# One block of sixteen value products per key tile instead of two of eight, in a two-layer conditioned attention on one Trainium2 core

## What is computed

```python
xn = layer_norm(x, norm_w, norm_b)
q = (xn @ q_w + q_b).reshape(Bx, Tx, H, -1)
k = (xn @ k_w + k_b).reshape(Bx, Tx, H, -1)
att = jnp.einsum('bnhl,bmhl->bnmh', q, k)
att = att + (1.0 - mask) * -1000000.0
att = jax.nn.softmax(att, axis=2)
v = ((xn @ v_w + v_b) * src_mask[:, :, None]).reshape(Bx, Tx, H, -1)
y = jnp.einsum('bnmh,bmhl->bnhl', att, v).reshape(Bx, Tx, Dx)
```

## Time and profile before

| | us |
|---|---|
| median of 3 runs | 675.45 |
| lowest and highest | 674.78, 677.27 |
| span of the profiled execution, first to last instruction | 674.4 |
| PE busy | 589.8 (87%) |
| DVE busy | 470.1 (70%) |
| ACT busy | 347.5 (52%) |
| POOL busy | 53.5 (8%) |

### The profile page before, as it was taken

How to read it: one execution, slowest core, us unless ns; L and a number is a source line. 1 busy time by engine, 2 the same in 40 slices (tenths; PEclk the granted TensorE clock), 3 DMA queues, 4 the chain that set the end, 5 groups by cost and what they waited for, 6 DMA issues and landing times.

```text
span 674.4 us, 9341 instructions
## 1 busy us (share of the span) xinstructions
PE 589.8 (87%) x2922; PEld 241.6 (36%) x2922; DVE 470.1 (70%) x905; ACT 347.5 (52%) x409; POOL 53.5 (8%) x42
## 2 busy tenths in 40 slices
PE   1989888999999999999999999999889666999666
PEld 1464412222222222222222222222234553588655
DVE  4639996888788788788888788888020547585652
ACT  1565304564655656656656655656976421538021
POOL 7224600000000000000000000000000005000000
PEclk9999955999999999999999999999989896999969
DMA  8188801500600600600410330100000000000003
GB/s 228 51 142 205 338 21 31 65 0 4 96 1 3 95 0 3 93 2 3 70 25 3 52 43 3 57 7 3 2 1 1 0 0 1 0 1 1 0 1 124
DMA packets 20021, 29.95 MB, mean 44 GB/s; under 512 B 5202, under 2 KB 11556, under 8 KB 19844
## 3 DMA queue, kind: packets, MB, share of 16 engines
q1 hardware_dynamic: 19996, 29.62, 20.8%
HBM read 21.02 MB, written 8.60 MB: 44 GB/s over the span
## 4 chain that ended last, share of the span: by engine, by line
PE 62%; DVE 23%; ACT 9%; issue 4%; DMA 1%; SPq 0%; DVEq 0%; ACTq 0%
PE bank L539 18%; PE bank L519 15%; DVE halfmax L749 15%; PE bank L500 14%; PE bank L581 11%; ACT work L391 3%; DVE stats L708 2%; ACT work L425 2%; DVE y_all L788 1%; PE bank L552 1%; DVE work L722 1%; DVE parts L722 1%; PE bank L524 1%; ACT parts L408 1%; DMA vecs<-in_mask_BxS_ff 1%
## 5 line engine op out<-in xcount | busy, mean ns | idle before, releaser
L749 DVE TENSOR_REDUCE halfmax<-bank 128x1 f32<-128x512 f32 x512 | 325.7, 688 | 63.7 <-PE bank L519 63.5
L425 ACT ACTIVATE work<-bank 128x1024 f32<-128x1024 f32 x256 | 250.0, 1023 | 152.6 <-PE bank L581 152.3
L519 PE MATMUL bank<-ks,qs 99*128 (+1 forms) x512 | 202.9, 404 | 17.1 <-DVE halfmax L749 11.0
L581 PE MATMUL bank<-qs,ks 102*128 (+1 forms) x512 | 167.6, 386 | 7.9 <-ACT work L425 5.4
L539 PE MATMUL bank<-work,vs 128*32 128x512 f32 x1024 | 137.0, 608 | 0.4 <-ACT yT L433 0.4
L519 PEld LDWEIGHTS bank<-ks,qs 99*128 (+1 forms) x512 | 49.7, 97 | 228.4 <-DVE halfmax L749 125.3
L581 PEld LDWEIGHTS bank<-qs,ks 102*128 (+1 forms) x512 | 47.5, 100 | 61.2 <-ACT work L425 18.5
L500 PE MATMUL bank<-parts,work 128*128 128x256 f32 x192 | 44.6, 393 | 7.1 <-ACT work L391 7.1
L500 PEld LDWEIGHTS bank<-parts,work 128*128 128x128 f32 x192 | 37.7, 198 | 13.4 <-ACT work L391 7.6
L367 POOL COPY vs<-v_all 128x512 f32 (+1 forms) x8 | 4.9, 612 | 396.8 <-PE bank L539 396.8
L500 PE MATMUL bank<-work,y_all 128*128 128x512 f32 x64 | 30.9, 624 | 2.4 <-ACT work L391 2.4
(11 more groups left out here) (119 smaller groups left out, 406.1 us busy)
## 6 DMA issues: line engine op xcount, KB each, us to landing
part_rows<-parts SPq DMA_DIRECT2D x8, 768.0 KB, 5.0
qs<-part_rows SPq DMA_DIRECT2D x48, 128.0 KB
ks<-part_rows SPq DMA_DIRECT2D x48, 128.0 KB
xs<-in_x SPq DMA_DIRECT2D x2, 1024.0 KB, 6.1
out_x<-xs SPq DMA_DIRECT2D x4, 512.0 KB, 2.9
parts<-in_L_cond_emb_w SPq DMA_DIRECT2D x1, 1024.0 KB, 5.6
parts<-in_L_cond_W_emb SPq DMA_DIRECT2D x1, 1024.0 KB, 7.9
ks<-in_mask_BxSx_fk SPq DMA_DIRECT2D x1, 1024.0 KB, 4.8
```

The lines of the kernel that those rows point to most:

```text
L425: act.activation(prob[:, c % 2, j, :], sT[u % 2][:, :], ACT.Exp).then_inc(exp_done, 1)
L519: pe.matmul(o, qs[0:ROW_MAX, slot, j, qt * P:(qt + 1) * P], ks[0:ROW_MAX, slot, j, n * HALF:(n + 1) * HALF], start=True, stop=True).then_i ...
L581: last = pe.matmul(sT[u % 2][:, n * HALF:(n + 1) * HALF], ks[0:ROWS, slots[0], j, c * P:(c + 1) * P], qs[0:ROWS, slots[0], j, n * HALF:(n ...
L749: dve.tensor_reduce(halfmax[:, r, n:n + 1], src, axis=AX.X, op=ALU.max, negate=True).then_inc(sN_read, 1)
```

## The change

The value products of both query halves of a tile are now issued together, after head 1, as one block of eight source matmuls (sixteen MATMUL records). The turns that went with the two blocks go with the one: 4 before it, 4 after it. The number of instructions, their operands and the `pv_done` increment stay the same.

```diff
-                        if c > 0 and j % 2 == 1:
-                            turns(VALUES_TURNS // 2)
-                            values(g, c - 1, j // 2)
-                            turns(VALUES_TURNS // 2)
-                        if c == 0 and not first and 1 <= j <= NH:
-                            turns(VALUES_TURNS // 2)
-                            values(g - 1, NT - 1, j - 1)
-                            turns(VALUES_TURNS // 2)
+                        if j == 1 and (c > 0 or not first):
+                            turns(VALUES_TURNS // 2 * NH)
+                            for n in range(NH):
+                                values(g if c > 0 else g - 1, c - 1 if c > 0 else NT - 1, n)
+                            turns(VALUES_TURNS // 2 * NH)
```

## The result

| | before | after |
|---|---|---|
| median | 675.38 (4 runs) | 717.36 (4 runs) |
| lowest and highest | 674.78, 677.27 | 717.25, 721.62 |
| span of the profiled execution | 674.4 | 715.7 |

The ratio after to before is 1.063, with a 95% interval of 1.0599 to 1.0662. The change costs 42 us; 39.6 were forecast.

The account below looks back on a forecast made before the run. A loop through PE and DVE, closed by two banks, was taken to bound the kernel. Terms 24.0 + 6.2 + 5.4 + 4 = 39.6 us took the span from 674.4 to about 714, the median to 715; range 701 to 725.

Parts of the forecast that it names:

- What bounds the kernel: Middle of the attention: a loop through PE and DVE, closed by two banks, 3.09 us per half tile; exponentials cost nothing.
- What is taken away: Value blocks: one of sixteen saves PE 0.25 us per tile, about 15 us over 63 tiles if PE were the bound.
- The stepping: Adding start-to-start prices from the trace through each tile's order: middle groups of 57.7 us against 52.9 before.
- The two waits: In each tile S waits for exponentials, some 40 us in all, and F for its bank, some 20 us longer.
- The mean of 0.77 for a bank's return: From the start of a DVE reduction to the F it frees: 0.84 or 0.72 us, taken as 0.77.
- The 1.08: From the start of an exponential to the S two units on: 1.08 us, read from one place.
- The sum: Whole kernel: 24.0 for five middle groups, 6.2 for the first, 5.4 for group 6, 4 for group 7: 39.6 us.
- Group 7: Last group, without F: tiles go from 4.25 to 5.04 us, those with conditioning products from 5.73 to 5.97; +4 in all.
- the tile of the y transposes: In the last group: waits for DVE's layer norm anyway, so costed at nothing; without that cover it adds 1.1 us.
- The one on the other side, faster through the saved drain: Attention: PE alone sets the pace, so 0.25 us for each of 63 tiles is saved, about 660 us; chance 4%.
- Rival 3: Attention: only one wait bites, +9 us (about 684) without ACT's price or +26 (about 701) without DVE's; 13% together.
- rival 4: Attention: more waiting lowers PE's clock, tiles cost 10 us and more, and the time passes 850 us; chance 2%.

Follow-up runs that it names:

- Quick maxima: The kernel before with each reduction of maxima over 64 columns in place of 512: 618.27 us.
- quick exponentials: The kernel before with exponentials of 256 columns in place of 1024 in the attention of layer 0: 669.14 us.
- both quick: Exponentials of 256 columns and reductions over 64, in each order: 612.67 us in the kernel before, 611.85 in the changed one.
- merge_last: The kernel before with the value blocks merged in group 7 alone, which has no F: 679.77 us against 675.49, ratio 1.0061.
- a_max: The changed kernel with each reduction of maxima over 64 columns in place of 512: 659.57 us.
- one_spread: The kernel before with the value blocks merged after head 1, but the F left in their old places: 698.47 us against 676.48, ratio 1.0322.

## Why the prediction was right, and where it was off

**What bounds the kernel.** Right. Quick maxima take 6.0 us off each middle group of the kernel before, quick exponentials 0.25. With both quick a group takes 46.7 and not 53.3. So the loop through PE and DVE sets the pace, not PE's work and not ACT.

**What is taken away.** Right: the block of sixteen takes 1.92 and frees PE at 1.86, and by PE's steps 0.24 us are saved for each tile, where 0.25 was forecast. In the time it never shows, as the waits take more. That holds even with both helpers quick: the waits of a middle group grow from 0.1 to 2.4 us for the 1.8 that are saved, 1.3 of them in F behind F, and the group takes 47.02 against 46.74. The stepping had put these waits at some 11 us in all, 0.17 for a tile, where they are 0.29, and so expected -4 where -0.8 came out. In the profiled spans the difference is -1.8, and the stage ahead of the attention, with the same instructions, makes -2.0 by itself.

**The two waits.** Right in kind and place: S of the third and fourth unit waits for the exponential, the third F of a row waits for its bank. They were a little too small. In the tile shown the third F starts 314.06 - 312.80 = 1.26 after the first of the row, and the last F 318.60 - 317.34 = 1.26 after its own; the sum has 1.19. The waiting S starts 315.85 - 314.70 = 1.15 after its exponential's start; the sum has 1.08.

The mean of 0.77 for a bank's return was about right. The last section shows that it is mostly 0.83 for one bank of the ring and 0.74 for the other, and the changed kernel waits for both. The 1.08 was too small: of 86 S that wait so from 121 to 473 us in the changed kernel, 69 start 1.15 us or more after the exponential's start, and 13 under 1.10. It had been read from a single place, ahead of 116 us, where an S lasts 0.61 and not 0.38. The middle groups came out at +5.43 and not +4.8; that this price makes most of the 0.6 is likely, but no run shows it by itself.

The waits before S had been forecast at some 40 us in all, and those before F at 20 more. The page has 28.6 before S, 20.7 more than before, and 21.7 more before F. But the page counts such a wait only from the modelled end of the matmul ahead; by the steps in the table, the changed kernel waits 4.2 more for each middle group before S and 3.3 more before F.

**The sum.** The total is 2.4 us off (42.0 measured, 39.6 forecast), and its parts are off by more, both ways. Groups 1 to 5 came out at +27.2, not 24.0. The first group, up to POOL's first copy, came out at +5.9, not 6.2. Group 6, copy to copy, went from 45.63 to 52.58, +7.0, not 5.4. Group 7 had been put at +4; from POOL's last copy to the start of the last value block it went from 42.07 to 43.19, +1.1. A part of this shift is where the copy cuts, as it now comes one unit of group 7 sooner (0.7 us). The larger part is the tile of the y transposes. It had been costed at nothing, because it "waits for DVE's layer norm anyway"; it shrank from 9.18 to 6.61. The rows under `merge_last` show what it waited for, an exponential behind ACT's table loads. In the changed kernel the block and the transposes come first:

```profile
527.98 1.92 PE L539 MATMUL bank<-work,vs 128*32 128x512 f32 x16
529.84 1.09 PE L524 MATMUL bank<-ident,yT 128*128 128x128 f32 x8
...
532.22 0.61 PE L581 MATMUL bank<-qs,ks 102*128 102x512 bf16 x2 [0.86 <-ACT work L425]
```

The last value block itself took 1.5 longer, at a lower clock, and the layers behind it 1.4 less, with the same instructions. Together this is the span's +41.3. That the total came so close is in part luck: group 7 is 2.9 under its forecast, groups 1 to 6 are 4.7 over theirs.

**The rivals.** The one on the other side, faster through the saved drain, fell: its point of decision was a wait under 0.25 us in a tile, and the tile shows 0.44, 0.54 and 0.36. Rival 3, that one of the waits alone bites, fell too, but the runs make each wait alone dearer than it had them. They are +14 for the bank and +41 for the exponentials, where it had +9 and +26 with the other helper at no cost at all; for the cuts as they were run, the stepping had +10.3 and +36. The clock's fall, rival 4, did not happen in the middle of the attention, where the clock is 1.00; short falls stand in the last group, in the kernel before as well.

**The rules of the Trainium skill.** That a change of tiling mode drains TensorE (TensorEngine Tiling (Array Packing), Tiling Modes, Key Properties) agrees with the rows: PE is free 1.86 after the start of one block of sixteen, and 1.00 after each block of eight. In the time it was not to be had. The warning of the Trainium skill's same page (Performance Considerations, PSUM Bottleneck) pointed the right way, as the readers of PSUM decided. But it speaks of readers that a faster TensorE outruns. Here they stand idle while the one block runs, DVE for 1.47 us, and have to be caught up with after it.

## What to carry to other kernels

A block of work on one engine is also the cover under which its partners catch up. Before merging two such blocks, step through one period with the start-to-start distances from the trace and see what each partner finds to do during the longer block, given how many buffers it has: with two banks DVE had 1.3 us of work for a block of 1.9. A total that fits can hide parts that do not: set each part against its own stretch of the trace, as the last group here shows. When the spacing decides, the same stepping, set against a trace first, can also find a better spacing than the one at hand.

## What was not expected of the hardware

**The clock fell in the last group, behind waits under 1 us.** The last value block, the same sixteen instructions, lasts 1.92 us in the kernel before and 3.44 in the changed one, behind a wait of 0.81 for an exponential. The stretches (columns as in the earlier trace rows) show the granted clock: 1.00 up to the wait and 0.55, mostly the level of 1.2 GHz, in the block.

```profile
562.78 3.44 PE L539 MATMUL bank<-work,vs 128*32 128x512 f32 x16 [0.81 <-ACT work L425]
```

```profile
545.00:562.70 17.70, 16.35 (x118) 8.55 (x118) 0.62 (x7) 11.24 (x12) 0.00 (x0) 1.00 0.00 0
562.70:566.50 3.80, 3.44 (x16) 0.59 (x16) 0.23 (x2) 0.26 (x2) 0.00 (x0) 0.55 0.00 0
```

`merge_last` has the same in its last block (3.58 us). Ahead of the fall stood conditioning products of two columns each, two units of scores, more such products, and the wait. But the wait alone does not bring it. In `a_max` the same block behind the same wait runs at full clock:

```profile
504.80 1.92 PE L539 MATMUL bank<-work,vs 128*32 128x512 f32 x16 [0.81 <-ACT work L425]
```

In `one_spread` the clock fell earlier in that group, behind a wait of 0.31; these two matmuls take 1.04 and not 0.60, and the block behind them 2.92:

```profile
520.98 1.04 PE L581 MATMUL bank<-qs,ks 102*128 102x512 bf16 x2 [0.31 <-ACT work L425]
```

The clock was 0.81 over 23 us there, and the tiles with conditioning products took 6.36, 6.92 and 6.36 where the same order took 5.93 in the changed kernel; with the tile after them that is 3.1 us.

```profile
521.90:545.00 23.10, 21.67 (x133) 9.41 (x132) 0.86 (x8) 10.61 (x11) 0.00 (x0) 0.81 0.00 0
```

The kernel before has such a fall too, in the tile of the y transposes behind the wait of 2.57 us. No run was made to find which of these things brings the clock down.

**The two banks of the ring have different prices.** From the start of a reduction to the F that it frees there are two values, and they go by the bank. From 121 to 473 us in the changed kernel 145 F behind an F or an S start later than a plain step would have them. Of the 64 in the second bank, which takes keys 512 to 1023, all start 0.74 to 0.75 after the start of their reduction. Of the 81 in the first, 65 start 0.81 to 0.84 after it. Whether PE stood idle or the matmul ahead still ran makes no difference: of the 64, PE stood idle before 53 and not before 11. In the tile shown above the reduction that starts at 317.11 freed the F whose weights are loaded here, 0.74 after it, with PE idle ahead of it:

```profile
317.85 0.10 PEld L519 LDWEIGHTS bank<-ks,qs 99*128 x1 [0.42 <-DVE halfmax L746]
```

Bank and half of the keys always go together in this kernel, so the runs cannot say which of the two it is. For a mean, 0.79 serves; for one step of a loop, the price of its own bank should be put into the sum.
